# Moving the lines and values of the second batch into the attention of the first

## What is computed

```
x = x + 0.5 * ffn(layernorm(x))        # 16 experts, 2 of them per token, and a shared one
x = x + attention(layernorm(x))
x = x + 0.5 * ffn(layernorm(x))

attention(x):                           # 16 heads
    x_bigram = [x, x shifted by one token]
    L_q = exterior(x_bigram @ W1_q, x_bigram @ W2_q)   # 6 numbers a head, of two 4-vectors, norm 1
    L_k = exterior(x @ W1_k, x @ W2_k)
    scores = (L_q . J6 L_k) * 6 ** -0.5, causal; softmax
    v = x @ W_v + b_v                   # 16 numbers a head
    return (softmax(scores) @ v) @ W_o + b_o
```

## Time and profile before

| | |
|---|---|
| median of 3 runs | 1398.82 us (1396.91 to 1401.12) |
| the profiled execution | 1399.43 us |
| its span, first to last instruction | 1397.7 us |
| PE, ACT, DVE, POOL busy in the span | 1074.4, 886.4, 789.4, 544.6 us |
| TensorE's granted clock, mean | 0.908 of full speed |
| first part (`ffn`) | to about 280 us |
| lines and values | 280 to 457 us |
| attention's groups | 457 to 1026 us, last projections to about 1044 us |
| last part (`ffn`) | to the end |

### The profile page before, as it was taken

How to read it: one execution, slowest core, us unless ns; L and a number is a source line. 1 busy time by engine, 2 the same in 40 slices (tenths; PEclk the granted TensorE clock), 3 DMA queues, 4 the chain that set the end, 5 groups by cost and what they waited for, 6 DMA issues and landing times. The chain is left out here.

```text
span 1397.7 us, 25164 instructions
## 1 busy us (share of the span) xinstructions
PE 1074.4 (77%) x7328; PEld 556.8 (40%) x7328; DVE 789.4 (56%) x1361; ACT 886.4 (63%) x1264; POOL 544.6 (39%) x576
## 2 busy tenths in 40 slices
PE   3998999837774788888887888788859989999300
PEld 1455899724553111222121212221124557999200
DVE  6797576658998315252535243433446993766433
ACT  1423677635663999998987989789834324777100
POOL 1169766366646112111211020202000488666475
PEclk9999999959886899999998989899978999999655
DMA  6900355645654101111110010101007502555454
GB/s 217 285 8 16 116 169 166 136 120 165 191 157 135 62 27 35 32 30 29 34 38 26 27 35 27 37 9 45 1 2 223 164 0 58 167 167 162 105 161 143
DMA packets 123113, 130.26 MB, mean 93 GB/s; under 512 B 12712, under 2 KB 109712, under 8 KB 123024
## 3 DMA queue, kind: packets, MB, share of 16 engines
q1 hardware_dynamic: 109200, 91.34, 21.0%
q0 software_dynamic: 13824, 37.77, 10.5%
HBM read 78.73 MB, written 50.33 MB: 92 GB/s over the span
## 5 line engine op out<-in xcount | busy, mean ns | idle before, releaser
L1475 ACT ACTIVATE attn_attend_probs<-banks 128x1536 f32<-128x1536 f32 (+1 forms) x448 | 507.6, 1277 | 61.0 <-PE banks L1398 60.3
L1419 PE MATMUL banks<-attn_attend_probs,attn_attend_v_now 128*32 128x512 f32 (+3 forms) x2560 | 314.3, 572 | 0.0
L1487 POOL TENSOR_SCALAR_AFFINE_SELECT attn_attend_probs<-attn_attend_probs 128x512 f32<-128x512 f32 (+2 forms) x176 | 88.1, 516 | 497.7 <-ACT attn_attend_probs L1475 497.1
L1398 PE MATMUL banks<-attn_attend_q_now,attn_attend_k_now 32*128 32x512 f16 (+3 forms) x1280 | 163.7, 365 | 94.1 <-ACT attn_attend_probs L1475 85.2
L639 POOL DMA_INDIRECT f_region<-xn_rows,f_token_of x160 | 158.6, 991 | 87.1 <-PE banks L500 83.1
L1398 PEld LDWEIGHTS banks<-attn_attend_q_now,attn_attend_k_now 32*128 32x128 f16 x1280 | 43.0, 91 | 372.7 <-ACT attn_attend_probs L1475 334.1
L511 PE MATMUL banks<-f_xnt 128*128 128x128 f32 x1280 | 171.1, 277 | 2.1 <-ACT f_xnt L593 1.1
L511 PEld LDWEIGHTS banks<-f_xnt 128*128 128x128 f32 x1280 | 155.4, 191 | 6.9 <-issue 3.9
L588 ACT ACTIVATE f_xnt<-f_w_all 128x514 f32 x160 | 101.2, 632 | 59.7 <-issue 55.9
L1502 DVE COPY attn_attend_sums<-banks 128x512 f32<-128x512 f32 x32 | 22.0, 688 | 186.0 <-PE banks L1419 185.7
L1521 DVE TENSOR_TENSOR x_res<-banks,x_res 128x512 f32 (+1 forms) x32 | 22.1, 691 | 165.6 <-PE banks L1431 165.5
(11 more groups left out here) (206 smaller groups left out, 1535.1 us busy)
## 6 DMA issues: line engine op xcount, KB each, us to landing
y_slots<-f_xnt SPq DMA_DIRECT2D x160, 128.0 KB
xn_rows<-f_stage SPq DMA_DIRECT2D x16, 512.0 KB, 3.1
attn_v<-attn_lines_v_out SPq DMA_DIRECT2D x32, 256.0 KB, 3.1
attn_attend_v_now<-attn_v SPq DMA_DIRECT2D x32, 256.0 KB, 2.9
x_res<-L_attn_x SPq DMA_DIRECT2D x8, 512.0 KB, 7.6
f_w_all<-L_ffn_We SPq DMA_DIRECT2D x2, 2048.0 KB, 13.6
f_w_all<-L_ffn_be SPq DMA_DIRECT2D x2, 2048.0 KB, 15.5
attn_q<-attn_lines_q_out SPq DMA_DIRECT2D x8, 512.0 KB, 3.1
```

Source lines behind the costliest of these rows:

```text
L1398: last = pe.matmul(score[i % SLOTS][:, j, c0:QW], k_now[rows, kt * P:(kt + 1) * P], q_now[rows, qc * QW + c0:(qc + 1) * QW], start=True, s ...
L1419: last = pe.matmul(out_bank[qc][rows, c0:QW], v_now[:, kt, rows], probs[:, place_of[HG * u + h], c0:QW], start=(kt == 0), stop=(u == last_ ...
L1475: act.activation(probs[:, at:at + n, c0:QW], score[i % SLOTS][:, 0:n, c0:QW], ACT.Exp, scale=SCALE).then_inc(sem.exp_done, 1)
L1487: pool.affine_select(out=part, in_=part, compare_op=ALU.is_ge, fill=0.0, base=0, pattern=[[0, end - begin], [1, P]], channel_multiplier=-1 ...
```

## The change

Stage one keeps the four blocks of the first batch (`EARLY = BLOCKS // 2`), all steps written out. The four blocks of the second batch are cut into pieces, and piece by piece they are put behind strips of the first four groups: block 4 + g in group g. Those pieces use one PSUM bank, bank 5, one after another, and no ACT: what ACT did for a block is done by DVE (copies out of PSUM, normalization, doubling), and the two roots become a power of -0.5 on POOL. To free bank 5, the strips of groups 0 to 3 alternate between three pairs and two. All eight groups are written out. POOL fetches for block 4 and 5 and adds the biases of the first four blocks in the last two steps of stage one; its other fetches and biases are pieces within groups. SP loads each chunk of group 0 as soon as its block is stored. `probs` is a ring of 20 places instead of 24, and a diagonal unit is masked by one instruction.

The core of the diff:

```diff
+EARLY = BLOCKS // 2
...
+    def is_early(n, lag):
+        return 0 <= n - lag < EARLY
+
+    def early_steps(emit, lag):
+        for n in range(EARLY + lag):
+            emit(n, n % 2, n // 2)
...
         def step(n, q, r):
+            if is_early(n, 0):
                 for j in range(BT):
+                    fetch(pool, n, j)
             halves(n - 1, 1 - q)
+            if n in (EARLY, EARLY + 1):
+                for j in range(BT):
+                    fetch(pool, n, j)
                 pool.wait_ge(sem.b_ready, 1)
+                for b in (2 * (n - EARLY), 2 * (n - EARLY) + 1):
+                    add_bias(pool, b)
...
+        def turn(pe, n, c):
+            k = of_late(n)
+            pe.wait_ge(late.staged, k + 1)
+            if c == 1:
+                pe.wait_ge(late.xt_ready, DC * k + 1)
+            elif k > 0:
+                pe.wait_ge(late.copied, 4 * k)
+            for j in range(BT):
+                last = pe.transpose(one_bank[:, j * P:(j + 1) * P], stage[:, n % 2, j, c * P:(c + 1) * P], core.ident[:])
+            last.then_inc(late.turned, 1)
...
+        def project_now(pe, n, j):
+            k = of_late(n)
+            pe.wait_ge(late.xt_ready, DC * (k + 1))
+            if j > 0:
+                pe.wait_ge(late.points_ready, BT * k + j)
+            pe.matmul(one_bank, xt[:, 0, 1 + j * P:1 + (j + 1) * P], w_now[:, 0, :], start=True, stop=False)
...
+        def turn_feats(pe, n, i):
+            k = of_late(n)
+            pe.wait_ge(late.feats_ready, k + 1)
+            if i == 0:
+                pe.wait_ge(late.points_ready, BT * (k + 1))
+            else:
+                pe.wait_ge(late.copied, 4 * k + i)
...
+        def invert_size(pool, n):
+            pool.wait_ge(late.size_ready, of_late(n) + 1)
+            pool.tensor_tensor(inverse[:], size[:], minus_half[:].to_broadcast([P, 2 * BT * H]), ALU.pow).then_inc(late.inverse_ready, 1)
...
+        def keep_feats(dve, n, i):
+            k = of_late(n)
+            side, pair = i // 2, i % 2
+            if pair == 0:
+                dve.wait_ge((sem.q_stored, sem.k_stored)[side], 16 * n)
+            dve.wait_ge(late.feats_turned, 4 * k + i + 1)
+            buf = (q_out, k_out)[side]
+            dve.tensor_copy(buf[:, 2 * pair:2 * pair + 2, :].rearrange("p g n -> p (g n)"), one_bank.bitcast(FP16)).then_inc(late.copied, 1)
...
-    SLOTS, RING, WIDE = 2, 8, 3
+    SLOTS, RING, WIDE = 2, 20, 3
...
+    narrow, full = Plan(units, (WIDE, WIDE - 1), RING, 2 * WIDE * QW), Plan(units, (WIDE, WIDE), RING, 2 * WIDE * QW)
+    plan = [narrow] * GROUPS + [full] * GROUPS
+    proj_steps = {0: {38: (QC - 1, 0), 41: (QC - 1, 1)}, 1: {39: (0, 0), 42: (0, 1), 51: (1, 0), 56: (1, 1), 61: (2, 0), 66: (2, 1)}}, \
+        {0: {30: (QC - 1, 0), 34: (QC - 1, 1)}, 1: {30: (0, 0), 34: (0, 1), 44: (1, 0), 47: (1, 1), 51: (2, 0), 54: (2, 1)}}
...
+    turn_steps, now_steps, rest_steps, feats_steps = [13, 15], [18, 25, 30, 35], [19, 27, 33, 38], [59, 64, 68, 69]
+    fetch_steps, other_steps, inverse_step, bias_step, deviation_step = [24, 26, 28, 30], [39, 40, 41], 45, 50, 66
+    measure_step, split_step, combine_steps, sums_step, normalize_step = 40, 52, [57, 61], 65, 1
...
-        with eng.Fori(1, ALL // 2) as two:
-            for side in range(2):
-                emit(two * 2 + side, side, two)
+        for g in range(ALL):
+            emit(g, g % 2, g // 2)
```

More of the change, by code:

```diff
@@ L1293, in attend @@
-    width = [n * (QW - c0) + STRIP_COST for _, n, c0 in strips] * 2
-    begins = [sum(width[:i]) for i in range(2 * N + 1)]
-    pv_step = [next(i for i in range(2 * N) if begins[i] >= begins[last_strip[u] + 1] + PV_LAG) for u in range(U)]
-    pv_at = {i: [u for u in range(U) if pv_step[u] == i] for i in range(max(pv_step) + 1)}
-    for i in range(N):
-        assert pv_step[(strips[i][0] + strips[i][1] - 1) // HG] <= i + RING - 2
-    pieces = []
-    for u in diagonal:
-        runs = []
-        for h in range(HG):
-            at = place_of[HG * u + h]
-            if runs and runs[-1][1] == at:
-                runs[-1][1] = at + 1
-            else:
-                runs.append([at, at + 1])
-        pieces.append(runs)
@@ L1386, in scores @@
         def scores(g, i):
[L1387 to L1391 removed]
+            first, n, c0 = plan[g].strips[i]
+            for qc in range(QC):
+                if first <= HG * (last_of[qc - 1] + 1 if qc else 0) < first + n:
+                    pe.wait_ge(q_loaded[qc], 16 * (g + 1))
+                    pe.wait_ge(kv_loaded[qc], 32 * (g + 1))
             if later(g) or i >= SLOTS:
[L1393 removed]
+                pe.wait_ge(sem.exp_done, base[g] + i - SLOTS + 1)
+            if g == GROUPS and i == 1:
+                pe.wait_ge(late.semaphores.copied, 4 * EARLY)
             for j in range(n):
@@ L1426, in project @@
             before = projected_before(two, qc, half)
[L1427 removed]
+            if before > 0:
                 pe.wait_ge(sem.proj_added, before)
@@ L1490, in gpsimd, with mask, lines_piece @@
-        groups(pool, group)
+        def mask(g, u):
+            c0, at = units[u][2], HG * u % RING
+            pool.wait_ge(sem.exp_done, base[g] + plan[g].last_strip[u] + 1)
+            pool.sem_inc(sem.mask_turn, 1)
+            part = probs[:, at:at + HG, c0:c0 + P]
+            pool.affine_select(out=part, in_=part, compare_op=ALU.is_ge, fill=0.0, base=0,
+                               pattern=[[0, HG], [1, P]], channel_multiplier=-1).then_inc(sem.masked, 1)
+        def lines_piece(n, i):
+            if i in fetch_steps and n + 2 < BLOCKS:
+                late.fetch(pool, n + 2, fetch_steps.index(i))
+            if i in other_steps:
+                late.other_products(pool, n, other_steps.index(i))
+            if i == inverse_step:
+                late.invert_size(pool, n)
+            if i == bias_step:
+                late.add_bias(pool, n)
+            if i == deviation_step and n + 1 < BLOCKS:
+                late.invert_deviation(pool, n + 1)
@@ L1492, in vector @@
+        def group(g, side, two):
+            for i in range(plan[g].N):
+                for u in diagonal:
+                    if plan[g].last_strip[u] == i:
+                        mask(g, u)
+                if g < GROUPS:
+                    lines_piece(EARLY + g, i)
+        late.invert_deviation(pool, EARLY)
+        groups(group)
     def vector(dve):
```

496 lines of the change are left out of this document (349 added, 147 removed).

## The result

The change made the kernel slower: 1418.9 us median of 4 runs (1417.45 to 1420.04) against 1398.76 for the kernel before on the same chip, a ratio of 1.0143 [1.0124, 1.0161].

The account below looks back on a forecast made before the run. ACT was taken to bound attention before (90% and 88% busy), PE groups 0 to 3 after. First exponential -72, groups 0 to 3 +59, groups 4 to 7 -8 sum to -21: 1378 us from 1398.8, range 1346 to 1406.

Parts of the forecast that it names:

- First exponential: Start of attention: four blocks fewer before it put the first exponential at 385.2 instead of 457.56 us, -72 (-76 to -66).
- Groups 0 to 3: First four attention groups, which take in the moved blocks: 85 us each, 340 against 281, +59 (+31 to +91).
- PE budget of 75 us a group: PE's work in each of groups 0 to 3: 59.5 us for attention with the new strips plus 13.0 and 2.1.
- the sum with 10 us idle: Groups 0 to 3: 75 us of PE work, 10 idle and half a microsecond of lowered clock, taken as 85 a group.
- Named waits: Groups 0 to 3: the shared bank makes PE wait about 1.7 us at steps 13 and 15, 1.8 at 68 and 69.
- Narrow strips: Groups 0 to 3: 70 strips a group instead of 56 cost ACT +0.6 us a group, at most 2.2.
- Groups 4 to 7: Last four groups: no loop jump (5.2 us) and projections off the shortest strips (3) give 280 against 288, -8 (0 to -14).
- DVE: Groups 0 to 3: DVE has some 54 of 85 us of work a group, a bound only in order, not in sum.
- Better cover: Rival: PE's idle in groups 0 to 3 shrinks to 3 us, 78 a group, 1350 us in all; chance 0.20.
- the full payment of interleaving: Within the better-cover rival: groups stay at 70 us despite the moved blocks and the kernel comes to 1319 us.
- DVE's order with the bias beside: Rival: in groups 0 to 3, steps 40 to 57, POOL delays DVE; decides from 90 us a group, 93 gives 1410; chance 0.13.
- Late start: Rival: something else gates attention, the first exponential comes at 405 instead of 385 us, result 1398; chance 0.07.

Follow-up runs that it names:

- half power: The changed kernel with POOL's power over 64 of the 128 columns, the other half of the inverse left as it stood: ratio 0.9875 to the kernel before.
- a lighter PE: The changed kernel with a difference for the power and one of four matrix products left in the late blocks' projections: ratio 0.9711 to the kernel before.
- the root by steps: The changed kernel with POOL's power replaced by shifted bits and three Newton steps on DVE, eleven short instructions: ratio 0.9915 to the kernel before.

## Why the prediction was wrong

**The step that failed** is the inventory of what the change adds. The text of the change says that the two roots become a power on POOL, and the prediction priced it nowhere. DVE's 27 us a block and PE's 13 stand in the sum, and POOL's 3.1 + 2.7 us in the rival that adds up its work; the power was in effect put at nothing, and with it the wait of the feature transposes for it. The runs showed 20.75 us on POOL in each of groups 0 to 3, which PE waited for up to 14.9 us, and 53.8 us off the four groups when a difference stood in its place. No row of before shows a power, so it needed a bound, and the nearest rows would have been a guess either way: ACT's root of this tile takes 0.31 us, POOL's product of 128 columns 0.85. Priced from those it would still have been thought hidden. What the prediction could have had is a wide upper end and a rival, since no row held the price. And since DVE has the chain to itself from `size` to the features, with PE's transposes fixed behind strip 59, it could have said how much delay the cover holds: 7 us of chunk and additions on DVE's side and a few more until strip 59. The half power shows it: 10.5 us hide in groups 1 to 3. Beyond that nearly every microsecond is PE's, and ACT's.

**The other steps, one by one.**
- *First exponential*: -72 forecast, -71.1 measured. Right, and by the route forecast: POOL's first two bias additions end at 367.5 (forecast 366.6), its products at 370.3 (369.7), and the tail behind them is 15.6 us (15.5). DVE's own products were held by POOL's additions meanwhile, 5.98 us for one that otherwise takes about 1, but DVE was only 0.6 us later than POOL with them, so it hardly showed:

```profile
363.77 5.98 DVE L1221 TENSOR_TENSOR attn_lines_line<-attn_lines_points 128x384 f32<-128x384 f32 x1 [3.80 <-ACT attn_lines_points L1135]
```

- *Groups 0 to 3*: 340 forecast; 391.8 measured, 338.0 with the power taken out. The PE budget of 75 us a group is met (301.65 / 4 = 75.4 busy in that run), and so is the sum with 10 us idle. Its reading, that PE is the bound, fits: three quarters of a lighter PE came off the time, with the bank's turns shortened too. The rest is order: moving five pieces, with the work unchanged, gave 2.9 us a group on average.
- *Named waits*: steps 13 and 15 at 1.7 us, 68 and 69 at 1.8. Measured in the changed kernel 1.5, 1.0, 0.0 and 2.1 at strip 16 and 1.6 to 1.8 at strip 70, and gone when moved. Right, but for the new gaps that the move made.
- *Narrow strips*: the +0.6 us for ACT was the smaller part of what they cost; alone they cost 3.5 us a group, near the 4.0 of the budget for PE (59.5 against 55.5).
- *Groups 4 to 7*: -8 (0 to -14) forecast, -20.3 measured. The mechanism was right and the size off: writing out alone gives -13.5 there, where the 5.49 us jump was all that was counted. By group it is 2.4, 6.7, 2.4 and 1.9: the second jump's stop lies in the second of them, and the rest is time behind the jumps and at later strips. Behind the first jump the granted clock is 0.81 for 22 us, then 1.00. The new plan gives 7.0 instead of 3. The Trainium skill (Runtime: NRT & Kernel Launch, Instruction fetch mechanics) says that a taken branch to code outside of the window already fetched stalls until that is fetched; the jumps' idle time of the earlier trace rows and its disappearance agree, and the trace doesn't show the fetch.
- *DVE*: "some 54 of 85 us"; busy 44.5 to 53.4 a group, right. SP's stores hid as expected: no wait for keys or values shows in groups 0 to 3.

With the power hidden the forecast of 1378 would have met 1366 (before 1398.65), off by the term for groups 4 to 7.

**The rivals.** *Better cover* (1350) didn't come, nor did the full payment of interleaving. The Trainium skill (Perfetto Trace Analysis, Optimization Strategy) says only that interleaving such regimes may improve performance; here, with the power out of the way, a group takes 84.5 us, not 70, and the whole is faster all the same. *DVE's order with the bias beside*: the outcome passed its deciding point, 98 us a group, by another mechanism. Its mechanism exists and its price was 2.1 us, once a group; in the changed kernel removing it took 8.6 us off strip 60 in four groups and nothing off the whole that could be seen, in the kernel with the root by steps it was worth 12 us in four groups, since there an addition that PE waits for stands behind it. *Late start*: no.

## What to carry to other kernels

List every operation that moves to another engine and price it there, even one that was cheap where it was: an instruction's cost belongs to the pair of operation and engine. Where no row shows the pair, work out how much delay its reader can take, and if that is a few microseconds, give the case a chance. And when a fault is mended, look at what now runs earlier: with the power gone, a bias addition that nobody waits for moved in front of an instruction that PE's bank hung on.

## What was not expected of the hardware

- POOL's power costs 0.16 us a column of 128 partitions (10.54 us for 64, 20.75 for 128), and 0.33 fixed, where its product of 128 columns takes 0.85. ACT's root of the 128 columns takes 0.31.
- Beside POOL's bias a DVE instruction with two inputs doesn't merely slow down: it stands until that ends and then takes most of its own time (3.02 or 3.10 us is what was left of POOL's 2.35 or 2.33, and 0.8; alone it takes 0.96). A small one stands as long. In the kernel after, just ahead of attention, an addition of four columns, 0.15 us otherwise, took 3.65 and ended with POOL's second bias, at 387.0. The timelines of POOL and DVE:

```profile
382.33 4.66 POOL L1011 TENSOR_TENSOR x_res<-x_res,attn_lines_b_o 128x1024 f32<-128x1024 f32 x2
...
383.38 3.65 DVE L1374 TENSOR_TENSOR attn_lines_mean<-attn_lines_parts 128x4 f32<-128x4 f32 x1
...
386.95 0.15 DVE L1375 TENSOR_TENSOR attn_lines_gap<-attn_lines_parts 128x4 f32<-128x4 f32 x1
```

  The Trainium skill (SBUF — State Buffer, Who interferes with whom) has the ports that DVE and POOL share as an exclusive lock, and a DVE instruction with two SBUF inputs as contending for it; these rows agree. One thing goes beyond it. Where POOL's instructions follow one another, DVE sometimes gets in between and sometimes not: here the second bias kept it out, and so did a second bias and two products in the row at 363.77 above (DVE ended at 369.75, the bias at 367.49), while in the kernel before, beside the four additions at 416.88 of the earlier trace rows, DVE's instructions at 417.20 and 420.23 took 3.00 and 2.98 us, each held by one addition, and POOL's second addition took 3.06. What decides that isn't shown.
- The power doesn't hold DVE at all, though it reads SBUF too. In the row at 546.34 above, 6 us into POOL's 20.76, a DVE addition of two inputs in SBUF took the 0.69 us that it takes everywhere; all 6 such instructions of chunks that ran beside a power in groups 0 to 3 took 0.69 or 0.75 as elsewhere. So the power cost what it did by its length and DVE's wait for its result, not by the ports.
- The loop jump costs more than its visible stop: writing out gave 13.5 us in groups 4 to 7 where one stop of 5.5 us was seen. Part of the rest is the lower granted clock behind a jump, 0.81 for 22 us.
